# Latent attention on tiles of 32 rows and 32 columns, four heads at a time

## The reference

```python
q_blhd = jnp.einsum('bld,dhk->blhk', x_bld, Wq)                # 16 heads of 64
latent_bll = jnp.einsum('bld,dc->blc', x_bld, Wkv_down)         # 32 wide, shared by all heads
k_blhd = jnp.einsum('blc,chk->blhk', latent_bll, Wk_up)
v_blhd = jnp.einsum('blc,chk->blhk', latent_bll, Wv_up)
attn = jnp.einsum('bqhd,bkhd->bhqk', q_blhd, k_blhd) / jnp.sqrt(HD)
attn = jax.nn.softmax(jnp.where(mask, attn, neg_inf), axis=-1)  # causal
y_blhd = jnp.einsum('bhqk,bkhd->bqhd', attn, v_blhd)
return jnp.einsum('bqhd,hdo->bqo', y_blhd, Wout)
```

## Time and profile before

| | us |
|---|---|
| median of 3 runs (2980.59 to 2983.26) | 2981.41 |
| the profiled execution | 2981.51 |
| its span, first to last instruction | 2979.5 |
| phase a2 in it, 1558.9 to 2126.2 | 567.3 |
| a2 until the first scores, at 1603.1 | 44.1 |
| one item of a2 in the steady part | 32.3 |

### The profile page before, as it was taken

How to read it: one execution, slowest core, us unless ns; L and a number is a source line. 1 busy time by engine, 2 the same in 40 slices (tenths; PEclk the granted TensorE clock), 3 DMA queues, 4 the chain that set the end, 5 groups by cost and what they waited for, 6 DMA issues and landing times. The chain is left out here.

```text
span 2979.5 us, 41067 instructions
## 1 busy us (share of the span) xinstructions
PE 2708.0 (91%) x16065; PEld 1255.3 (42%) x16065; DVE 1835.3 (62%) x2337; ACT 1181.8 (40%) x1607; POOL 1490.1 (50%) x932
## 2 busy tenths in 40 slices
PE   4899999999948999999948999999687999999968
PEld 3333333333324444444424444444333444444433
DVE  2577677777573666666573677677543566666653
ACT  2444444444413444444412444444222444444422
POOL 1577777777703555555602556556201555555520
PEclk8899999999957999999957999999895999999979
DMA  4000000000000000000000000000000000000000
GB/s 104 1 1 1 1 1 1 1 1 1 0 16 1 1 1 1 1 1 1 1 15 14 1 1 1 1 1 1 1 0 1 1 1 1 1 1 1 1 1 14
DMA packets 21345, 14.63 MB, mean 5 GB/s; under 512 B 3233, under 2 KB 20001, under 8 KB 21026
## 3 DMA queue, kind: packets, MB, share of 16 engines
q1 hardware_dynamic: 21154, 12.01, 1.6%
HBM read 9.91 MB, written 2.10 MB: 4 GB/s over the span
## 5 line engine op out<-in xcount | busy, mean ns | idle before, releaser
L777 POOL TENSOR_TENSOR sums<-sums,p 128x1024 f32<-128x1024 f32 (+3 forms) x704 | 1367.9, 1943 | 730.5 <-PE ps L550 652.2
L692 DVE TENSOR_REDUCE half_max<-ps 128x2 f32<-128x1024 f32 (+3 forms) x640 | 696.9, 1089 | 547.0 <-PE ps L531 499.8
L507 PE MATMUL ps<-q,k 64*128 64x512 f32 (+3 forms) x3328 | 754.9, 532 | 0.0
L616 ACT ACTIVATE p<-ps 128x1024 f32<-128x1024 f32 (+3 forms) x704 | 585.3, 849 | 365.3 <-PE ps L510 198.9
L510 PE MATMUL ps<-max_row,pick 64*128 64x512 f32 (+3 forms) x1664 | 571.8, 684 | 0.0
L550 PE MATMUL ps<-p,v 128*64 128x512 f32 (+3 forms) x2816 | 565.8, 515 | 0.0
L712 DVE RECIPROCAL inverse<-total 128x128 f32<-128x128 f32 x512 | 477.7, 939 | 59.3 <-ACT total L657 48.9
L531 PE MATMUL ps<-k_near,q_near 64*128 64x512 f32 (+2 forms) x1664 | 369.6, 441 | 64.5 <-DVE half_max L692 47.9
L692 DVE TENSOR_REDUCE neg_max<-ps 128x2 f32<-128x256 f32 x192 | 158.6, 826 | 314.4 <-PE ps L536 314.4
L531 PEld LDWEIGHTS ps<-k_near,q_near 64*128 64x128 f32 x1664 | 160.9, 190 | 432.6 <-issue 281.4
L507 PEld LDWEIGHTS ps<-q,k 64*128 64x128 f32 x3328 | 293.3, 187 | 91.2 <-issue 66.3
(11 more groups left out here) (138 smaller groups left out, 2054.1 us busy)
## 6 DMA issues: line engine op xcount, KB each, us to landing
q_w<-in_wq SPq DMA_DIRECT2D x3, 512.0 KB
o_w<-in_wo SPq DMA_DIRECT2D x3, 512.0 KB
k_w<-in_wk SPq DMA_DIRECT2D x2, 512.0 KB
v_w<-in_wv SPq DMA_DIRECT2D x2, 512.0 KB
out<-x SPq DMA_DIRECT2D x4, 256.0 KB, 2.8
scratch<-in_wq_t SPq DMA_DIRECT2D x1, 512.0 KB, 5.3
scratch<-in_w_out SPq DMA_DIRECT2D x1, 512.0 KB, 7.6
wq_latent<-scratch SPq DMA_DIRECT2D x1, 512.0 KB, 3.3
```

The lines of the kernel that those rows point to most:

```text
L507: nc.tensor.matmul(out[:, head, 0:width], a.k[rows, key_slot(i, 3), k * P:(k + 1) * P], a.q[rows, i % 3, s * BANK + lo:(s + 1) * BANK], st ...
L616: act.activation(probabilities(g)[:, :, lo:BANK], score[g % 2][:, :, 0:BANK - lo], ACT.Exp)\
L692: last = v.tensor_reduce(out, chunk_ps[:, :, 0:hi - lo], AX.X, ALU.max, negate=True)
L777: pool.tensor_tensor(sums, sums, probabilities(g)[:, :, lo:BANK], ALU.add).then_inc(summed, 1)
```

## The change

a2 gets a function of its own, `latent_phase`; the other three attentions stay with `attention_phase`.

- Four heads share the 128 partitions, 32 rows each, with no padding. An item is four heads of one batch: 8 items.
- A unit is 256 queries; a step is two key tiles (256 keys) against it; an item has 10 steps. At the last step of a unit the second key tile has only 128 live queries, so a step has 512 or, at the diagonal, 384 columns for each head.
- `score` is one buffer of four banks, one per head. One ACT instruction takes the exponential of 2048 or 1536 columns.
- Each head's values and, as a second product, its row sums (the matrix `ones` as weights) come on 32 output rows, both into one bank: columns 0 to 255 and 256 to 511. POOL no longer adds, `total` and its copy are gone, and ACT's copy of the bank brings both.
- A chunk still serves two heads in two banks, so that four heads need two chunks: 20 per item, two per step, LEAD = 6.
- The causal masks are products of 32 columns each, four for every key tile and head, with new constants that POOL makes at the start of a0 (`shape_constants`).
- The multiplication by the inverse goes from DVE (L720) to POOL; two reciprocals of 128 columns per unit.
- `wq_latent` and `wo_latent` are half as large; the buffers of zeros in setup are gone.

```diff
+QUADS = H // 4
+QUADRANTS = tuple(slice(LATENT * n, LATENT * n + LATENT) for n in range(4))
...
-            sp.wait_ge(latent_copied, 3)
-            sp.dma_start(dram["wq_latent"].rearrange("n p c -> p n c"),
-                         m.scratch[:, 0:1024].rearrange("p (n c) -> p n c", c=P)).then_inc(latent_stored, 16)
-            sp.dma_start(dram["wo_latent"].rearrange("n p c -> p n c"), wo_eff).then_inc(latent_stored, 16)
+            sp.wait_ge(latent_copied, 2)
+            for name, made in (("wq_latent", wq_eff), ("wo_latent", wo_eff)):
+                sp.dma_start(dram[name][0:QUADS].rearrange("n p c -> p n c"), made.rearrange("p (n c) -> p n c", c=P))\
+                    .then_inc(latent_stored, 16)
...
+            if make_constants:
+                shape_constants(nc, pool, a, sem)
...
+def shape_constants(nc, pool, a, sem):
+
+
+    blank, shaped = sem("blank"), sem("shaped")
...
+    for rows in QUADRANTS:
+        pool.affine_select(out=a.tri_scores[rows], in_=a.tri_scores[rows], compare_op=ALU.is_ge, fill=MASKED, base=0,
+                           pattern=[[LATENT, 4], [-1, P]], channel_multiplier=1).then_inc(shaped, 1)
+        pool.affine_select(out=a.tri_chunk[rows], in_=a.tri_chunk[rows], compare_op=ALU.is_ge, fill=MASKED, base=0,
+                           pattern=[[-LATENT, 4], [1, P]], channel_multiplier=-1).then_inc(shaped, 1)
...
+def latent_phase(nc, m, a, tag, dram, after):
...
+        score, chunk_ps, mix, small = m.ps[:, 0:4, :], m.ps[:, 4:6, :], m.ps[:, 6, :], m.ps[:, 7, :]
+        SCALE = HD ** -0.5
+        QW = 256
+        UNITS = S // QW
+        ITEMS = H // 4 * B
+        LEAD = 6
+        SLOTS = 3
+        probs = a.p[:].rearrange("p (s g) h c -> p s (g h) c", s=SLOTS)
+
+        steps = [(s, n) for s in range(UNITS) for n in range(s + 1)]
+        NS = len(steps)
...
+            if s == 0:
+                groups = [[(t, 0, P, 0, 0), (u, 0, 2 * P, P, 0)]]
+            elif s == 1:
+                groups = [[(t, 0, 3 * P, 0, 0)], [(u, 0, 4 * P, 0, 0)]]
+            elif s == 2:
+                groups = [[(t, 0, BANK, 0, 0)], [(u, 0, BANK, 0, 0)],
+                          [(t, BANK, P, 0, 1), (u, BANK, 2 * P, P, 1)]]
+            else:
+                groups = [[(t, 0, BANK, 0, 0)], [(u, 0, BANK, 0, 0)], [(t, BANK, 3 * P, 0, 1)],
+                          [(u, BANK, 4 * P, 0, 1)]]
+            chunks += [(s, pair, group) for group in groups for pair in range(2)]
+        NC = len(chunks)
...
+        def tiles_of(s, n):
+
+            return [(2 * n, 0, 0), (2 * n + 1, QW, P if n == s else 0)]
+
+        def width(s, n):
+            return QW + P if n == s else 2 * QW
...
+        when = {("q", 0): -10, ("q", 1): -5, ("top", 0): -3, ("top", 1): -1, ("top", 2): 1, ("out", 0): 3,
+                ("top", 3): 4, ("out", 1): 6, ("out", 2): 8, ("out", 3): 12}
...
+            some = [c for c in range(PER_STEP * (g + LEAD), PER_STEP * (g + LEAD + 1)) if 0 <= c < CHUNKS_IN_ALL]
+            return some[:1], some[1:]
...
+            def scores(g):
+                i, s, n = step(g)
+                if g >= 1:
+                    pe.wait_ge(exped, g)
+                if n == 0:
+                    pe.wait_ge(small_out, use_of["top", i, s] + 1)
+                for k, at, lo in tiles_of(s, n):
+                    for head, rows in enumerate(QUADRANTS):
+                        nc.tensor.matmul(score[:, head, at:at + QW - lo], a.k[rows, i % B, k * P:(k + 1) * P],
+                                         a.q[rows, i % 3, s * QW + lo:(s + 1) * QW], start=at == 0, stop=False,
+                                         skip_group_check=True)
+                for k, at, lo in tiles_of(s, n):
+                    for head, rows in enumerate(QUADRANTS):
+                        last = nc.tensor.matmul(score[:, head, at:at + QW - lo], a.pick4[rows, :],
+                                                a.max_row[rows, s % 2, lo:QW], start=False, stop=True,
+                                                skip_group_check=True)
+                if n == s:
+                    for _, at, _ in tiles_of(s, n):
+                        for quarter in range(4):
+                            for head, rows in enumerate(QUADRANTS):
+                                lo = at + quarter * LATENT
+                                last = nc.tensor.matmul(score[:, head, lo:lo + LATENT], a.tri_scores[rows, quarter, :],
+                                                        a.unit32[rows, :], start=False, stop=True,
+                                                        skip_group_check=True)
+                last.then_inc(scored, 1)
+
+            def chunk(c):
+                i, (s, pair, parts) = c // NC, chunks[c % NC]
+                if c >= 1:
+                    pe.wait_ge(maxed, c)
+                if c % NC == 0 or s == 2:
+                    pe.wait_ge(rounded, round_of["q", i, s // 2] + 1)
+                    if i < B:
+                        pe.wait_ge(rounded, round_of["k", i, s // 2] + 1)
+                heads = [(head, QUADRANTS[2 * pair + head]) for head in range(2)]
+                for n, (t, lo, keys, at, _) in enumerate(parts):
+                    for head, rows in heads:
+                        last = nc.tensor.matmul(chunk_ps[:, head, at:at + keys], a.q_near[rows, i % 2, t * P:(t + 1) * P],
+                                                a.k_near[rows, i % B, lo:lo + keys], start=n == 0, stop=False,
+                                                skip_group_check=True)
+                for t, lo, keys, at, _ in parts:
+                    if lo + keys == (t + 1) * P:
+                        for quarter in range(4):
+                            for head, rows in heads:
+                                lo_column = at + keys - P + quarter * LATENT
+                                last = nc.tensor.matmul(chunk_ps[:, head, lo_column:lo_column + LATENT],
+                                                        a.tri_chunk[rows, quarter, :], a.unit32[rows, :], start=False,
+                                                        stop=True, skip_group_check=True)
+                last.then_inc(chunked, 1)
+
+            def mix_step(g):
+                i, s, n = step(g)
+                pe.wait_ge(exped, g + 1)
+                if n == 0:
+                    pe.wait_ge(mixed_out, unit(i, s))
+                    if i < B and s == 0:
+                        pe.wait_ge(small_out, use_of["v", i, 0] + 1)
+                for k, at, lo in tiles_of(s, n):
+                    for part in range(2):
+                        for head, rows in enumerate(QUADRANTS):
+                            what = a.ones[:, 0:LATENT] if part else a.v[:, i % B, k, 0:LATENT]
+                            last = nc.tensor.matmul(mix[rows, part * QW + lo:(part + 1) * QW], what,
+                                                    probs[:, g % SLOTS, head, at:at + QW - lo],
+                                                    start=k == 0 and part == 0, stop=n == s and at > 0,
+                                                    skip_group_check=True)
+                last.then_inc(weighed, 1)
...
+                    for t in range(2):
+                        last = nc.tensor.transpose(small[:, t * P:(t + 1) * P], a.neg_max[:, part % 2, t, :], m.ident[:])
...
+            for g in range(FIRST, END):
+                ahead, behind = chunks_at(g)
+                for c in ahead:
+                    chunk(c)
+                if 0 <= g < TOTAL:
+                    scores(g)
+                for use in uses_at.get(g, ()):
+                    use_small(*use)
+                for c in behind:
+                    chunk(c)
+                if 0 <= g - 1 < TOTAL:
+                    mix_step(g - 1)
...
+                act.activation(probs[:, g % SLOTS, :, 0:width(s, n)], score[:, :, 0:width(s, n)], ACT.Exp)\
+                    .then_inc(exped, 1)
...
+                act.activation(a.mixed_raw[:, u % 2, :], mix, ACT.Copy).then_inc(mixed_out, 1)
...
+                v.reciprocal(a.inverse[:, cols], a.mixed_raw[:, u % 2, QW + half * P:QW + (half + 1) * P])\
+                    .then_inc(inverted, 1)
...
+            inverts_at = {end_step(i, s) + 1: (i, s) for i in range(ITEMS) for s in range(UNITS)}
+            for g in range(FIRST, END):
+                ahead, behind = chunks_at(g)
+                for c in ahead:
+                    row_max(c)
+                if g in inverts_at:
+                    invert(*inverts_at[g], 0)
+                for n, kind, i, part in uses_at.get(g, ()):
+                    if kind == "out":
+                        add_out(n, i, part)
+                for c in behind:
+                    row_max(c)
+                if g in inverts_at:
+                    invert(*inverts_at[g], 1)
+
...
+                pool.tensor_tensor(a.mixed[:, 0:QW], a.mixed_raw[:, u % 2, 0:QW], a.inverse[:, 0:QW], ALU.mult)\
+                    .then_inc(normed, 1)
...
```

(17 more changed lines are left out.)

214 lines of the change are left out of this document (187 added, 27 removed).

## The result

The changed kernel takes 2819.4 us (median of 4 runs, 2815.0 to 2820.9), the kernel before 2981.6 beside it (2980.6 to 2983.3): ratio 0.9453, 95% interval 0.9437 to 0.9469. Forecast were 2821 us and a range of 2790 to 2900. The profiled execution took 2815.0 us with a span of 2813.3. Two later executions, one of the run `adjacent` (4035 us) and one of the kernel before beside it (5211 us), were in a slow state and enter no time or ratio given here.

What follows compares the result with a forecast made beforehand. PE was taken to bound the kernel: 43.0 us of PE work plus 1.6 of waits an item made a2 409 us instead of 567.3; with setup 1.8 shorter, 2981.5 became 2821 us, range 2790 to 2900.

Steps and rivals of the forecast that it cites:

- What bounds the kernel: In a2's steady part PE's queue sets the time: busy 31.52 of 32.31 us an item before the change.
- Scores and mixing: In a2, four 32-row or 32-column tiles run at once: scores 11.3 us, mixing 16.0 us an item.
- The size of PE's work: PE's products in an a2 item sum to 41.8 us, with 3% added 43.0 us.
- The waits: PE waits in an a2 item, from (a) and (b): 1.6 us, upper end 4.
- (a): Chunk to next chunk takes 1.79 us with its maximum; after a diagonal step PE's work is 0.17 short, four times.
- (b): A unit's two reciprocals of 0.94 us stand around the second maximum: 0.1 to 0.5 us in each of four steps.
- The start: The stretch of a2 before its first scores, eight projections and 13 chunks at about the low clock: 47 us.
- Less than fourfold: Rival: tiles in scores and mixing overlap only in part, 9 us more an item, 2896 us; chance 0.10.
- two tiles at a time: Rival: only two 32-wide tiles run at once in scores and mixing, 72.7 us an item, 3046 us; chance 0.04.
- the dear short products: Rival: a2's many short mask products cost more than their columns, 5.6 us an item, 2866 us; chance 0.06.
- the low clock: Rival: short, narrow products and waits keep a2's clock at 0.52, doubling PE's 43 us, 3165 us; chance 0.03.
- the maxima as the pace: Rival: DVE's queue is late at each a2 step, 48 us an item, 2848 us; inside the forecast's range.

Runs made afterwards that it cites:

- adjacent: Apparently the changed kernel with whole maxima and each step's second chunk moved right behind the scores on PE, DVE's order matched: 2823.7 us, median of three.
- two halving runs: Changed kernel with heads 2 and 3 on the tiles of heads 0 and 1: in the scores 2907.4 us, in the mixing 2935.8 us.
- short maxima: Changed kernel with a2's maxima over 32 keys only and reciprocals over 8 columns only: 2803.3 us, 44.43 us an item.
- reordering run: Kernel with short maxima, plus each step's second chunk moved right behind the scores, ahead of the small product: 2786.3 us, 42.31 us an item.

## Why the prediction was right

**What bounds the kernel** held: PE is busy for 44.52 of 44.57 us, and shorter work on DVE or ACT changes an item by 0.14 and 0.04 us.

**Scores and mixing** (11.3 and 16.0 us, all four tiles at once) held in their mechanism, by the two halving runs: +10.7 and +15.3 for forecast 11 and 16. The Trainium skill's figures of 3.07 and 2.38 for packs of tiles ("TensorE: Matmul & The Clock Gate", section "Measured speedup vs the span model") don't describe this kernel. By an estimate from them the item would have taken 8 us more; here a full step's scores take 4.57 us in one row tile and 1.19 in four, and halving the column tiles doubled the mixing.

**The size of PE's work** was wrong by a little: 43.0 forecast, 44.4 measured (44.43 with nothing waiting for DVE). By start-to-start distances over the ten steps of an item with short maxima, chunks and scores take 21.4 us for 11.3 + 9.1, mixing 16.9 for 16.0, small products 6.1 for 5.4: 2.6 us above the bare sum of 41.8, of which the 3% covered 1.2. Diagonal mixing is the clearest: 1.43 for 1.28. I put the excess down to the gaps at the 40 changes of kind in an item, which the prices from the kernel before held only in part, and to tiles that stand idle around them; this is argued from the timeline, and the reordering run supports it without dividing it up.

**The waits** (1.6 us an item) were wrong by as much the other way: 0.14. The step of the prediction that failed is the waits (a) and (b): a distance of 1.62 against a chain of 1.79 was called 0.17 short. But a chunk that starts late costs PE only if nothing loaded before it is still running, and the true distances are longer, by the 2.6 us above, than those with which I compared the chain. That 43.0 + 1.6 = 44.6 is so near the measured 44.57 is luck: one error of +1.4 and one of -1.5 us an item, some 11 us each over the eight items, cancel. (Two slips in the working changed nothing: a distance of 1.73 was called covered against a chain of 1.79, and the break-even item of 64.8 us comes to 64.6.)

**The masks** took 2.8 for 3.4 us. **The start** took 40.96 us for 47: the chunks wait for the maxima as forecast, but the projections ahead ran at full clock for 10 us. In PE's timeline of the changed kernel four of five of the first products with 512 columns take 1.1 us, for 2.07 at the low clock; in the kernel before only the first did.

```profile
1560.47 1.12 PE L977 MATMUL ps<-xn_t,q_w 128*128 128x512 f32 x2 [0.69 <-ACT k L1029]
1562.29 1.13 PE L977 MATMUL ps<-xn_t,k_w 128*128 128x512 f32 x2 [0.69 <-ACT q L1029]
...
1567.25 2.07 PE L977 MATMUL ps<-xn_t,k_w 128*128 128x512 f32 x2 [0.47 <-ACT v L1031]
```

Why the clock stood high there in one and not in the other isn't settled; in the run with POOL's additions and the one-operand join the first scores came after 44.3 us. **The end** took 6.2 us for 7, **setup** gave 1.56 for 1.8. In all a2 took 401 us for 409, below the 405 to 420 named as a sign of being right, and the stretch behind it took 2.9 us longer at a lower clock (0.58 for 0.66 in its first part): 2815.0 in the profiled execution for 2821. A full step's scores, 1.19 us, missed their sign, within 1.15, by 0.04.

**The rivals.** Less than fourfold, two tiles at a time and the dear short products are refuted by runs; the low clock by the windows (1.00 in the steady items), though the run with one row tile shows that narrow products can bring it; the maxima as the pace, by short maxima.

## What to carry to other kernels

Float32 products on four 32-row or 32-column tiles ran side by side when they were issued in turn (a full step's scores took 1.19 us in four row tiles, 2.27 in two and 4.57 in one), so padding heads of 32 to 64 costs half the array. A sum of prices needs a term for the places where the kind of tile changes (here gaps of some 0.1 us, which the runs don't price one by one), and products on few tiles are cheapest beside products that leave just those tiles idle. Before work goes to an idle engine, look which small instructions of its neighbour with two operands in SBUF stand on the path.

## What I had not expected

- A chunk that uses two row tiles was free (0.02 us) beside scores that use all four, if it needs the two that the chunk before left idle.
- With one 32-row tile at a time in the scores, PE busy for 100 of 100 us was granted a clock of 0.65; with two tiles at a time, 1.00.
- A DVE instruction on 8 columns with two operands in SBUF took 1380 ns beside POOL's additions, 174 without them, and 172 beside them with one operand.
- An order edit that gained 2.1 us an item with short maxima lost 1.5 with whole ones: the second chunk came 3.1 us an item later.
